# Linear attention and a mixture of experts: sums of weighted expert outputs on GpSimd, split key-value products, one coefficient transpose, a new order

## The reference, cut to what matters

```python
h = ln_c(x)                              # normalised over the 128 channels of a token
q, k, v = h @ Wq.T + bq, h @ Wk.T + bk, h @ Wv.T + bv        # 8 heads of 16
Q, K = elu(q) + 1, elu(k) + 1
den = 1 / (sum_d Q * cumsum(K, over heads) + 1e-10)
num = causal linear attention: o_t = Q_t @ sum_{s <= t} K_s^T V_s, per head
x = x + num * den
t = tokens(x); f = ln_t(t)
p = softmax(f @ gate_w + router_gamma); keep the two largest of 8
y = sum_e keep_e * (gam_e * (f @ expert_w[e] + expert_b[e]) + bet_e)
out = t + y                              # back to channels x tokens
```

## Time and profile before

| | |
|---|---|
| time, median of 3 runs | 754.41 us (754.3 to 756.66) |
| the profiled execution: time, span | 755.91 us, 754.1 us |
| TensorE busy, weight loads | 717.1 us (95%), 624.0 us (83%) |
| VectorE busy | 685.9 us (91%) |
| ScalarE, GpSimd busy | 409.9 us (54%), 397.8 us (53%) |
| chain that ended last | PE 91%, DVE 4%, POOL 2% |
| costliest groups | causal masks (L574) 184.9 us; `y_act` (L397) 159.4; expert products (L915 to L917) 124.0, 113.7, 113.5; y transposes (L933) 80.8 |

### The profile page before, as it was taken

The page is one execution under the profiler, slowest core; times in us unless marked ns, Lnnn a source line. Parts: engine busy times, 40 slices in busy tenths (PEclk is TensorE's granted clock), DMA queues, the critical chain, the costliest instruction groups (busy, mean ns, idle before and its releaser), DMA issues.

```text
span 754.1 us, 23195 instructions
## 1 busy us (share of the span) xinstructions
PE 717.1 (95%) x8137; PEld 624.0 (83%) x8137; DVE 685.9 (91%) x2550; ACT 409.9 (54%) x1261; POOL 397.8 (53%) x639
## 2 busy tenths in 40 slices
PE   4767999999999999999999999999999999999986
PEld 2666888888888888888888888888888888888875
DVE  4567999999999999999999999999999999999984
ACT  1122666655555666666665555555555555555544
POOL 5145555555555555555555555555555555555520
PEclk9769999999999999999999999999999999999999
DMA  5101111111111111111111111111111111111101
GB/s 129 33 15 30 42 40 35 37 40 37 39 37 42 42 42 42 42 42 42 42 42 42 42 42 42 42 42 42 42 42 42 42 42 42 42 30 29 30 16 29
DMA packets 60214, 30.29 MB, mean 40 GB/s; under 512 B 2160, under 2 KB 60176, under 8 KB 60176
## 3 DMA queue, kind: packets, MB, share of 16 engines
q1 hardware_dynamic: 60176, 29.79, 14.4%
HBM read 20.34 MB, written 9.44 MB: 39 GB/s over the span
## 4 chain that ended last, share of the span: by engine, by line
PE 91%; DVE 4%; POOL 2%; ACT 1%; issue 1%; DMA 1%; SPq 0%; DVEq 0%; ACTq 0%; POOLq 0%
PE bank L877 11%; PE bank L915 10%; PE bank L894 9%; PE bank L916 9%; PE bank L917 9%; PE bank L933 8%; PE bank L901 4%; PE bank L909 4%; PE bank L884 4%; PE bank L853 3%; PE bank L854 3%; PE bank L855 3%; PE bank L860 3%; PE bank L847 2%; PE bank L866 2%; PE bank L935 2%
## 5 line engine op out<-in xcount | busy, mean ns | idle before, releaser
L574 DVE TENSOR_TENSOR probs<-bank,tri 128x512 f32<-128x512 f32 x288 | 184.9, 684 | 10.2 <-PE bank L877 4.7
L397 ACT ACTIVATE y_act<-bank,scale 128x128 f32<-128x128 f32 x576 | 159.4, 383 | 2.5
L915 PE MATMUL bank<-e_high,x_high 128*128 128x512 f32 x288 | 124.0, 431 | 1.1 <-DVE o L803 1.1
L916 PE MATMUL bank<-e_low,x_high 128*128 128x512 f32 x288 | 113.7, 395 | 0.0
L917 PE MATMUL bank<-e_high,x_low 128*128 128x512 f32 x288 | 113.5, 394 | 0.0
L311 POOL TENSOR_TENSOR qn<-feat,rden 128x512 f32<-128x512 f32 x36 | 38.2, 1061 | 116.4 <-DVE rden L672 116.4
L416 ACT ACTIVATE x_high<-x 128x512 fp32r<-128x512 f32 x36 | 22.8, 633 | 137.0 <-DVE x L664 137.0
L592 DVE SCALAR_TENSOR_TENSOR y_dve<-bank,scale,y_dve 128x128 f32<-128x128 f32 x288 | 92.4, 343 | 0.0
L580 DVE SCALAR_TENSOR_TENSOR qkv<-bank,rstd,b_qkv 128x384 f32<-128x384 f32 x144 | 86.8, 605 | 5.1 <-POOL rstd L301 2.6
L387 ACT ACTIVATE k_odd<-bank,parity 128x512 f32<-128x512 f32 x36 | 24.7, 687 | 114.4 <-PE bank L860 114.4
L933 PE MATMUL bank<-ident,y_act 128*128 128x128 f32 x576 | 80.8, 273 | 1.6 <-ACT y_act L397 1.6
(11 more groups left out here) (139 smaller groups left out, 1764.5 us busy)
## 6 DMA issues: line engine op xcount, KB each, us to landing
x<-in_x SPq DMA_DIRECT2D x36, 256.0 KB, 3.3
x_res<-in_x SPq DMA_DIRECT2D x36, 256.0 KB, 3.2
out<-o SPq DMA_DIRECT2D x36, 256.0 KB, 2.4
beta_raw<-in_L_ffn_beta_w SPq DMA_DIRECT2D x1, 512.0 KB
e_raw<-in_L_ffn_expert_w SPq DMA_DIRECT2D x1, 512.0 KB
w_raw<-in_L_conv_Wkv SPq DMA_DIRECT2D x2, 64.0 KB, 2.4
b_qkv<-in_L_conv_bkv SPq DMA_DIRECT2D x1, 128.0 KB, 4.4
w_raw<-in_L_conv_Wq SPq DMA_DIRECT2D x1, 64.0 KB, 2.6
```

What stands on the lines that cost most here:

```text
L397: last = nc.scalar.activation(y_act[:, p, u, e], bank[EXPERTS_AT[u][0]][:, 128 * e:128 * e + 128], ACT.Copy, scale=scale[:, p, u, e:e + 1])
L574: return tt(probs[:, half, i].rearrange("p u e t -> p (u e) t"), bank[SCORES_AT[half][i]][:].rearrange("p (n t) -> p n t", t=T), tri[:].un ...
L915: mm(out, x1_high[:, p, u], e_high[:, w], start=True, stop=False)
L916: mm(out, x1_high[:, p, u], e_low[:, w], start=False, stop=False)
```

## The change

Five edits, and a new order of all instructions in a step.

1. **Halves added on GpSimd.** `y_act` holds four scaled outputs of a unit. GpSimd adds the last two to the first two (one addition of 128x256 for a unit, `add_halves`), and TensorE transposes two parts and `y_dve`, three instead of five.
2. **Key-value products of 64 x 64.** Each unit's 128x128 product becomes two of 64 x 64, for heads 0 to 3 and 4 to 7, side by side in the bank. The masked form is written by two instructions of 64 partitions.
3. **One coefficient transpose.** The coefficients of all four units lie in 128 columns and are transposed at once; the bias is then four products of 128 columns with rows (`bias_rows`) that are zero but for the unit's own. These rows are prepared with the weights, by further transposes and small copies.
4. **One more stage.** `LAGS = 7`. x is loaded in stage 0, rounded in stage 1 and transposed in stage 2; projections are in stages 2 (unit 0) and 3; scores are in stage 4, the values in 5, the experts in 6.
5. **Other PSUM banks** for nearly everything.

VectorE's instructions are otherwise the same, in another order. The core of the diff:

```diff
-LAGS = 6
+LAGS = 7
...
-AT = dict(x=4, kv=3, att=6, x1_a=6, x1_b=4, k=1, q=7, coef=0, out=1)
-PROJ_AT = (4, 0, 3, 2)
-SCORES_AT = ((3, 7, 2, 0), (0, 5, 6, 7))
-EXPERTS_AT = ((4, 2), (6, 5), (1, 1), (2, 3))
+AT = dict(x=2, kv=7, att=6, x1_a=5, x1_b=6, k=4, q=6, coef=3, out=7)
+PROJ_AT = (5, 5, 2, 3)
+SCORES_AT = ((2, 1, 4, 0), (2, 5, 3, 6))
+EXPERTS_AT = ((5, 0), (7, 1), (3, 4), (7, 0))
...
+SUMS = 2
...
-        coef3 = sb("coef3", [128, PAR, U, 3 * QUAD], F32R)
-        coef_t = sb("coef_t", [3 * QUAD, PAR, U * T], F32R)
+        coef3 = sb("coef3", [128, PAR, U, QUAD // EXPERTS, EXPERTS], F32R)
+        coef_t = sb("coef_t", [128, PAR, T], F32R)
+        bias_high = sb("bias_high", [128, EXPERTS], F32R)
+        bias_cols = sb("bias_cols", [128, U, U, QUAD // EXPERTS, EXPERTS])
+        bias_rows = sb("bias_rows", [128, U, 128], F32R)
...
+            def add_halves(p, u):
+
+                return tt(y_act[:, p, u, 0:2], y_act[:, p, u, 0:2], y_act[:, p, u, 2:4], ALU.add)
...
+                    need(pool, "y_act_1", n + 1)
+                    add_halves(p, 1).then_inc(S["y_sum_1"], 1)
...
+                dve.wait_ge(S["rest_pe"], 4)
+                turned = bank[WEIGHTS_AT[3]][:, 0:EXPERTS]
+                make(copy(bias_high[:], turned))
+                dve.wait_ge(S["rest_dve"], done[0])
+                for u in range(U):
+                    make(copy(bias_cols[:, u, u, 0:2], bias_high[:].bitcast(F32).unsqueeze(1).broadcast_to([128, 2, EXPERTS])))
+                    make(tt(bias_cols[:, u, u, 2], turned, bias_high[:].bitcast(F32), ALU.subtract))
+                assert done[0] == REST_COLS
+                dve.wait_ge(S["rest_pe"], 5)
+                make(copy(bias_rows[:].rearrange("p u d -> p (u d)"), bank[WEIGHTS_AT[0]][:]))
...
+            def masked_blocks():
+
+                new = bank[AT["kv"]][:, 0:64 * U].rearrange("p (u d) -> p u d", u=U)
+                for i in range(2):
+                    rows = slice(64 * i, 64 * i + 64)
+                    last = tt(kv_new[rows, :, rows], new[rows],
+                              pair_mask[rows].unsqueeze(1).broadcast_to([64, U, 64]), ALU.mult)
+                return last
...
-                    last = mm(bank[AT["kv"]][:, 128 * u:128 * u + 128], feat[:, p, u, 128:256], qkv[:, p, u, 256:384],
-                              start=True, stop=True)
-                return last
+                    for i in range(2):
+                        last = mm(bank[AT["kv"]][64 * i:64 * i + 64, 64 * u:64 * u + 64],
+                                  feat[:, p, u, 128 + 64 * i:128 + 64 * i + 64],
+                                  qkv[:, p, u, 256 + 64 * i:256 + 64 * i + 64], start=True, stop=True)
...
+                return transpose(bank[AT["coef"]][:, 0:T], coef3[:, p].rearrange("p u s e -> p (u s e)").bitcast(F32), ident[:])
+
+            def bias(p):
+
                 for u in range(U):
-                    last = transpose(bank[AT["coef"]][0:3 * QUAD, T * u:T * u + T], coef3[:, p, u].bitcast(F32), ident[:])
-                return last
-
-            def bias(p):
-
-                return mm(bank[AT["out"]][:], e_bias3[:], coef_t[:, p], start=True, stop=False, skip_group_check=True)
+                    last = mm(bank[AT["out"]][:, T * u:T * u + T], bias_rows[:, u], coef_t[:, p], start=(u == 0),
+                              stop=False, skip_group_check=True)
+                return last
...
 
                 out = bank[AT["out"]][:, T * u:T * u + T]
-                for e in range(4):
+                for e in range(SUMS):
                     mm(out, y_act[:, p, u, e], ident[:], start=False, stop=False, is_transpose=True,
                        skip_group_check=True)
                 return mm(out, y_dve[:, p, u], ident[:], start=False, stop=True, is_transpose=True,
...
+                    need(pe, "y_sum_0", n + 1)
+                    turn_y(p, 0).then_inc(S["y_turned_0"], 1)
+                    need(pe, "y_sum_1", n + 1)
                     need(pe, "y_dve_12", n + 1)
                     turn_y(p, 1).then_inc(S["y_turned_1"], 1)
-                    need(pe, "y_act_0", n + 1)
-                    turn_y(p, 0).then_inc(S["y_turned_0"], 1)
-                    need(pe, "y_act_3", n + 1)
```

More of the change, by code:

```diff
@@ L371, in _ @@
+                if g[2]:
+                    n, p = g[2].i, g[2].par
+                    need(pool, "x_moments", n + 1)
+                    deviation("x_eps", n, mv1[:, p], ve1, eps[:, 0], rstd1[:, p]).then_inc(S["x_rstd"], 1)
             steps(pool, step)
@@ new lines, in step @@
+                if g[4]:
+                    n = g[4].i
+                    need(dve, "den", n + 1)
+                    nc.vector.tensor_scalar(den[:], den[:], 1e-10, None, ALU.add).then_inc(S["den_eps"], 1)
+                if g[6]:
+                    n = g[6].i
+                    need(dve, "second", n + 1)
+                    tt(rank2[:], rank[:, 1], order[:], ALU.mult).then_inc(S["rank_b"], 1)
+                if g[5]:
+                    n, p = g[5].i, g[5].par
+                    need(dve, "values_1", n + 1)
+                    need(dve, "values_0", n + 1)
+                    dve.wait_ge(x_res_loaded[p], 16 * (g[5].half + 1))
+                    need(dve, "out", n - 1)
+                    tt(flat(x1, p), bank[AT["att"]][:], flat(x_res, p), ALU.add).then_inc(S["x1"], 1)
@@ new lines, in step @@
+                if g[4]:
+                    n = g[4].i
+                    need(dve, "kv", n + 1)
+                    need(dve, "state", n)
+                    masked_blocks().then_inc(S["kv_new"], 1)
+                if g[2]:
+                    n = g[2].i
+                    need(dve, "x_turned", n + 1)
+                    parts([bank[AT["x"]][:, T * u:T * u + T] for u in range(U)], bn).then_inc(S["x_parts"], 1)
+                if g[6]:
+                    n, p = g[6].i, g[6].par
+                    need(dve, "y_dve_20", n + 1)
+                    weigh(p, 2, 1).then_inc(S["y_dve_21"], 1)
@@ new lines, in step @@
+                if g[5]:
+                    n = g[5].i
+                    need(dve, "lgm", n + 1)
+                    stt(rank[:, 0], lgm[:], 0.0, order[:], ALU.is_ge, ALU.mult).then_inc(S["rank_a"], 1)
+                if g[6]:
+                    n, p = g[6].i, g[6].par
+                    need(dve, "y_dve_11", n + 1)
+                    weigh(p, 1, 2).then_inc(S["y_dve_12"], 1)
+                if g[4]:
+                    n = g[4].i
+                    need(dve, "scores_1", n + 1)
+                    causal(1, 3).then_inc(S["probs_13"], 1)
@@ L879, in scores @@
                 return last
-            def from_state(p):
-                for u in range(U):
-                    last = mm(bank[AT["att"]][:, T * u:T * u + T], state[:, U * p + u], q_t[:, p, u],
-                              start=(u == 0), stop=False, skip_group_check=True)
-                return last
             def values(p, half):
@@ L989, in step @@
                     values(p, 0).then_inc(S["values_0"], 1)
+                if g[3]:
+                    n, p = g[3].i, g[3].par
+                    if k is not None:
+                        need(pe, "x_parts", n + 1)
+                    project(p, 2).then_inc(S["proj_2"], 1)
+                if g[6]:
+                    n, p = g[6].i, g[6].par
+                    need(pe, "probs_03", n + 2)
+                    need(pe, "x1_low", n + 1)
+                    if k is not None:
+                        need(pe, "y_one_3", n)
+                        need(pe, "y_dve_32", n)
+                    experts(p, 0, 1).then_inc(S["experts_01"], 1)
+                    need(pe, "out", n)
+                    if k is not None:
+                        need(pe, "kv_new", n + 2)
+                    experts(p, 1, 0).then_inc(S["experts_10"], 1)
@@ L1051, in step @@
[L1051 to L1062 removed]
+                    experts(p, 3, 1).then_inc(S["experts_31"], 1)
```

806 lines of the change are left out of this document (384 added, 422 removed), and 19 rows, old and new, of the table names.

## The result

The changed kernel is slower: 782.72 us median (781.5 to 787.91, 4 runs) against 755.28 (754.3 to 756.66, 4 runs), a ratio of 1.037 [1.0328, 1.0415]. The forecast was 746, with a range of 734 to 772. The profiled execution took 787.91 us, 32.0 more than that of before; it is the slowest of its four, 5.2 us above their median, so the medians differ by 27.4 only.

A forecast was written before the change was run, and what follows sets the result against it. The prediction took TensorE to set the 19.22 us step with VectorE right behind, becoming the new bound. From the profiled 755.9 us, -14.6 for the period and +6 for the ends gave 747.3; less 1.5 to the median, 746, range 734 to 772.

The forecast's parts named there:

- the period: Steady step: VectorE's 18.61 us as floor plus short waits, 18.75 against 19.22; 0.47 gained over 31 intervals, -14.6 us.
- VectorE's own term: VectorE's masked key-value product becomes two instructions, 0.83 against 0.69 us: +0.13 a step (ends 0 and +0.61), 18.48 to 18.61.
- GpSimd holds VectorE: Rival, slower: running GpSimd additions stretch VectorE's small two-input instructions; one full catch a step costs 0.74 us, 769; chance 0.25.
- two-catch case: Within the rival GpSimd holds VectorE: two full catches a step give 792 us, left out of the range.
- three signs named for being wrong: Small two-input VectorE means above 0.3 us; VectorE waiting for scores_1 over 0.3 us a step; four bias products taking 0.9.
- VectorE has a wait nearby (probs_13 for scores_1) that swallows 0.3 us: Argument against the rival GpSimd holds VectorE: a VectorE wait at probs_13 absorbs 0.3 us of stalls.
- The terms of TensorE: TensorE per step: y transposes -0.87, coefficients -0.33, bias +0.16, key-value products -0.10; sum -1.14, leaving 18.1 us.
- GpSimd's addition: Four additions of 128x256 a step, 0.74 us each; GpSimd goes from 10.9 to 13.8 us and costs nothing unless late.
- The ends: Start and finish of the run: +8 for later turn and preparation, -2 at the finish; +6 us, between 0 and +12.
- The wait moves: Rival, same: the loop scale, ScalarE, q, scores_1, probs_13 is 0.3 us longer; period 19.05, 755 us; chance 0.15.
- VectorE runs full: Rival, faster: VectorE has no wait left and the ends cost nothing, 735 us; chance 0.13.
- The transposes aren't what ends the step: Rival: removing y transposes brings nothing to the step, leaving the time of the ends alone, 760 us; chance 0.02.

The follow-up runs named there:

- e8: Kernel before with one VectorE instruction moved one place: the mask probs_01 goes ahead of lg2; 772.68 us, ratio 1.0248.
- e9: Changed kernel with one more wait: GpSimd's addition for unit 0 waits for VectorE's lg; 746.66 us, 0.9868 of the kernel before.
- e2: Changed kernel without GpSimd's additions, TensorE transposing all four weighted parts and y_dve; 766.12 us, 1.012 of the kernel before.
- e4: Changed kernel with one more wait: x1_low on GpSimd waits for VectorE's lg2; 767.78 us, 1.0174 of the kernel before.
- e5: Changed kernel with the split of the key-value products and of their mask undone, no wait added; 749.64 us, 0.9925 of the kernel before.
- e6: Changed kernel with e3's three waits and e5's whole key-value products together; 747.69 us, 0.9912 of the kernel before.
- e3: Changed kernel with three GpSimd waits: addition of unit 0 for lg, of unit 3 for rank_a, x1_low for lg2; 745.74 us, 0.9871 of before.
- e1: Changed kernel with each GpSimd addition replaced by a tiny addition and a write-only memset of about the same length; 744.54 us, 0.985 of before.
- e7: Changed kernel without GpSimd's additions and with x1_low waiting for lg2 (e2 and e4 together); 758.29 us, 1.0038 of the kernel before.
- e10: e3 with a fourth wait: GpSimd's addition for unit 2 waits for rank_a too; 746.71 us, 0.9874 of the kernel before.
- e11: Changed kernel with two TensorE neighbours swapped, experts_31 ahead of experts_00, no wait added; 768.29 us, 1.0182 of the kernel before.

## Why the prediction was wrong

**The step that failed is the period:** "18.61 of VectorE with no wait at all is the floor" and 0.14 us more were to be all. The floor itself came out near (18.57), in part by luck (below, *VectorE's own term*); what was added to it was 1.59 us of stretched instructions, which the sum put at nothing. They are the mechanism of the rival *GpSimd holds VectorE*, which had a chance of 0.25 and ended at 769 because it counted one addition in full. Its two-catch case, 792, lay outside the range. Of the three signs named for being wrong the first came, means above 0.3 us; VectorE doesn't wait for scores_1 in the steady steps, and the bias takes 0.50. Three of its arguments failed:

- *Only additions were looked at.* The largest catch, lg2's (0.66), is by `x1_low`, which was there before. e8 shows that lg2 was one place away from GpSimd's `qk` product in the kernel before as well.
- *"VectorE has a wait nearby (probs_13 for scores_1) that swallows 0.3 us."* That held for a VectorE with slack. Where it is the bound, it comes late to everything and has no wait left; no wait of VectorE in the steady steps gave anything back.
- *Catches were counted as independent.* They are linked here: e9 frees three with one wait. They need not be: e2 and e8 have a single large catch, e4 has two. What the rival lacked was a case in which one catch brings further ones.

Whether lg is caught hung on less than 0.4 us (e5), which an estimate of two engines' orders with durations from another order can't settle. In hindsight its chance had to be larger, and its price that of several catches.

**The trigger was a gain on an engine that isn't the bound.** The split products save TensorE time (below), and this brought the addition of unit 0 ahead of lg. Undone, with their two masks and nothing else, the kernel is 33 us faster than the changed one (749.64 against 782.72).

**The terms of TensorE.** Its timeline in the changed kernel, around the key-value products, the bias and the y transposes:

```profile
325.86 0.69 PE L939 MATMUL bank<-qkv,feat 128*64 128x64 f32 x16
326.47 0.65 PE L891 MATMUL bank<-ident,x 128*128 128x128 f32 x4
...
331.16 0.67 PE L973 MATMUL bank<-coef_t,bias_rows 128*128 128x128 f32 x4
331.66 0.62 PE L904 MATMUL bank<-ident,feat 128*128 128x128 f32 x4
...
332.12 0.38 PE L982 MATMUL bank<-ident,y_act 128*128 128x128 f32 x2
332.34 0.27 PE L984 MATMUL bank<-ident,y_dve 128*128 128x128 f32 x1
332.45 0.38 PE L982 MATMUL bank<-ident,y_act 128*128 128x128 f32 x2
```

From start to start: bias 331.66 - 331.16 = 0.50, as taken. Three y transposes 332.45 - 332.12 = 0.33, 0.11 each, as taken. Key-value products 0.61 against 0.89, so -0.28 where -0.10 was taken, within the ends. The page that spoke against the split (the Trainium skill, TensorEngine Tiling (Array Packing), Key Properties) is not contradicted, as a drain may be in the 0.61; it did not decide. One small slip in the forecast's working: 8 x 0.12 is 0.96 and not 0.94, which moves only the upper end of this term, by 0.02.

**VectorE's own term.** The masked products take 327.53 - 326.65 = 0.88 us against 0.61, two of 417 ns:

```profile
326.65 0.85 DVE L611 TENSOR_TENSOR kv_new<-bank,pair_mask 64x256 f32<-64x256 f32 x2
327.53 0.89 DVE L590 BATCH_NORM_STATS2 bn<-bank 128x6 f32<-128x128 f32 x4
```

+0.27 where +0.13 was taken. That the floor still came out near 18.61 is luck: of the 20.05 us of VectorE's busy time 1.59 are stretches, and without these and the +0.27 all other work takes 18.19, against the 18.48 of before that the sum carried over. Busy time counts the tail of the last instruction ahead of each wait, and most waits are gone; that this is the 0.29 is likely but not shown. The engine that became the bound pays nearly what the other saves: the split is worth 0.10 us a step (e6 against e3), and without the three waits it costs 33 us.

**GpSimd's addition** takes 0.74 us where nobody holds it, as taken from both sides; its busy time in a step is 14.1 us (forecast 13.8).

**The ends.** Taken as +6. Profiled time less 31 periods is 755.9 - 595.8 = 160.1 before and 787.9 - 625.0 = 162.9 after, +2.8; the variants with the same preparation have less (e9: 747.0 - 589.0 = 158.0, e1: 742.4 - 588.7 = 153.7). By the medians it is 159.5 before and 157.7 after, -1.8, since the profiled execution of the changed kernel lies 5.2 us above the median. So the ends cost nothing: the term was mis-sized by 3 to 8 us, and lies at the lower end of the forecast's 0 to +12 or a little below. The first projection came at 30.36 us against 26.52, 3.8 later where 4.6 + 3.5 was taken, and at 26.8 to 30.5 in the variants with the same preparation. The first `o`, "near 97", came at 94.52, at 93 in e2 and e7, and at 86 to 90 in the others; why is open.

**How near the forecast's own case was.** With the three catches gone (e9) the kernel takes 746.66 where 746 was said, but by two errors that cancel: a period of 19.00 where 18.75 was said (31 x 0.25 = +8), and ends of about -2 instead of +6. Of the 0.43 us over the floor of 18.57 in e9, the stretched rests (lgm 357 ns, lg2 246, rank_a 225: 0.29 over 0.18) are the greater part. e10 did not get them away, and what would is open.

**The other rivals.** *The wait moves* needs the loop through ScalarE to be late: in the changed kernel VectorE waits nowhere for it, only e11 made it so (0.46 at `probs_13`). *VectorE runs full* is e9 in kind, without the catches (busy for 18.82 of 18.97 us), but at 19.00 and not at 18.61. *The transposes aren't what ends the step* is ruled out: the wait before `o` went with them.

**The best versions** are e3 (745.74) and e9 (746.66), equal within their intervals; both beat the kernel before by 1.3% and the changed one by 4.6 to 4.9% (e9: 746.66 / 782.72 = 0.954; by the ratios to before, which take out the chip, 0.9868 / 1.0372 = 0.951).

## What to carry to other kernels

Before an engine that shares a lock becomes the bound, list every two-input instruction of it against every reading instruction of the other engine, old ones included, within 1 us in both lists: slack absorbs such a meeting only in part (e8: 0.81 us held, 0.54 lost), and at the bound one of them can make the engine late for the next. Look for the first meeting of the chain in the groups (a mean far above that of its twins), and guard it with a single wait on the engine with slack; here this cost nothing and gave 1.16 us of 20.16. A saving on an engine that isn't the bound isn't free either, if it moves a third engine's work into such a meeting.

## What the runs showed of the hardware

- A GpSimd instruction that only writes does not hold VectorE: in e1 six instructions on 128x32 with both inputs in SBUF lie wholly inside memsets of 630 ns and take 0.18 to 0.19 us. The Trainium skill (SBUF — State Buffer, SBUF: two separate sides) says that it takes a GpSimd instruction that reads SBUF; e1 agrees.
- GpSimd's instruction that waits for the port goes ahead of VectorE's next one: lg, queued directly behind `feat_1`, lost to the addition that had been ready since 329.09, 0.34 us before lg's record starts, and so in all 20 steps. With a lead of 0.01 us (e5) the addition didn't hold lg.
- The hold is until the GpSimd instruction's end: 128x32 instructions of 0.18 us took up to 0.99 (e8) and 1.01 us (e2). Larger VectorE instructions met none in the steady steps.
- Sixteen passes of 64 columns on half the array take 0.61 us, 38 ns each, against 111 ns for each of eight passes of 128 columns.
- A VectorE product of 64 partitions x 256 from PSUM takes 417 ns; two cost 0.88 us to the next instruction's start, more than one of 128 x 512 with its 0.61.
